# A graph network layer: projection and second neighbour sum made one stage, in the order of the places of the nodes

## The reference

```python
def _sage_conv(x, src, tgt, W_l, b_l, W_r):
    n = x.shape[0]
    msgs = x[src]
    agg = jax.ops.segment_sum(msgs, tgt, num_segments=n)
    deg = jax.ops.segment_sum(jnp.ones((src.shape[0],), x.dtype), tgt, num_segments=n)
    agg = agg / jnp.maximum(deg, 1.0)[:, None]
    return agg @ W_l + b_l + x @ W_r
h = jax.nn.relu(_sage_conv(x, src, tgt, W_l1, b1, W_r1))
logits = _sage_conv(h, src, tgt, W_l2, b2, W_r2)
```

## Time and profile before

| | us |
|---|---|
| three runs | 2976.88, 2973.86, 2979.23 |
| median | 2976.88 |
| profiled execution, own time | 2971.24 |
| its span in the trace | 2969.0 |
| PE busy in the span | 2485.4 |
| DVE busy | 2065.8 |
| POOL busy | 1809.9 |
| ACT busy | 779.7 |

### The profile page before, as it was taken

One profiled execution on the slowest core, in us unless ns is written; L12 is line 12 of the kernel. 1 busy time (PEld: TensorE's weight loads), 2 busy tenths in 40 slices (PEclk: granted clock), 3 DMA queues, 4 the chain that ended last, 5 costly groups with the idle time before them and its releaser, 6 DMA issues. The chain is left out here.

```text
span 2969.0 us, 35216 instructions
## 1 busy us (share of the span) xinstructions
PE 2485.4 (84%) x8644; PEld 1445.1 (49%) x8644; DVE 2065.8 (70%) x4653; ACT 779.7 (26%) x2019; POOL 1809.9 (61%) x1880
## 2 busy tenths in 40 slices
PE   5478888799999999989998858888777777787899
PEld 2133334245555555546666545555343444443577
DVE  8999999977777777744535656666654444444888
ACT  1011111067777767743222310000010000000232
POOL 4777776767676767740037757777547777777200
PEclk8789999889999999999999979999888777776799
DMA  9212222469999999982057665556343333333001
GB/s 267 84 56 77 83 72 87 149 183 267 265 268 263 264 267 263 267 247 95 26 154 201 201 195 169 168 169 169 96 135 106 105 106 106 105 106 105 22 1 45
DMA packets 238393, 446.46 MB, mean 150 GB/s; under 512 B 47451, under 2 KB 129005, under 8 KB 237999
## 3 DMA queue, kind: packets, MB, share of 16 engines
q0 software_dynamic: 96288, 254.83, 32.3%
q1 hardware_dynamic: 136416, 184.09, 19.0%
q10 hardware_dynamic: 5488, 5.28, 0.6%
HBM read 320.06 MB, written 126.13 MB: 150 GB/s over the span
## 5 line engine op out<-in xcount | busy, mean ns | idle before, releaser
L1746 POOL DMA_INDIRECT nbr_yg<-y_d,gidx x763 | 721.9, 946 | 243.6 <-PE nbr_sum L1856 124.9
L1856 PE MATMUL nbr_sum<-nbr_yg,nbr_hot 128*128 128x258 f32 x1526 | 599.9, 501 | 221.9 <-DMA nbr_yg<-y_d,gidx 175.2
L1794 DVE TENSOR_TENSOR nbr<-nbr_sum,nbr 128x258 f32 x763 | 323.5, 424 | 434.0 <-PE nbr_sum L1856 415.0
L855 POOL DMA_INDIRECT qg<-q_d,rb x480 | 480.0, 1000 | 205.5 <-DVE hb L941 102.8
L1856 PEld LDWEIGHTS nbr_sum<-nbr_yg,nbr_hot 128*128 128x128 f32 x1526 | 297.6, 231 | 507.7 <-DMA nbr_yg<-y_d,gidx 198.2
L410 POOL DMA_INDIRECT recs_d<-recs,slot_src x416 | 409.5, 984 | 164.4 <-issue 130.2
L972 PE MATMUL p_sum<-hb,wide 128*96 128x512 f32 x960 | 450.8, 591 | 0.1
L901 ACT ACTIVATE hb<-hb 128x512 f32<-128x512 f32 x480 | 296.7, 630 | 202.2 <-DVE hb L941 199.3
L941 DVE TENSOR_TENSOR hb<-p_h,qg 128x512 f32<-128x512 f32 x480 | 312.4, 680 | 26.5 <-DMA qg<-q_d,rb 21.6
L1244 POOL DMA_INDIRECT n_ahead<-y_d,gidx x165 | 158.1, 958 | 265.6 <-DMA y_d<-n_y 198.6
L698 PE MATMUL acc<-col_hot,lane_hot 128*128 128x464 f16 x832 | 205.2, 409 | 117.1 <-DVE lane_hot L645 117.1
(11 more groups left out here) (320 smaller groups left out, 3381.7 us busy)
## 6 DMA issues: line engine op xcount, KB each, us to landing
agg_d<-agg SPq DMA_DIRECT2D x240, 192.4 KB, 5.4
msg_d<-n_ahead SPq DMA_DIRECT2D x165, 128.0 KB, 2.9
nbr_ys<-msg_d SPq DMA_DIRECT2D x165, 128.0 KB, 2.7
nbr_yg<-y_d,gidx POOLq DMA_INDIRECT x763, 2.8
p_low<-p_d SPq DMA_DIRECT2D x11, 768.0 KB, 12.3
recs_d<-fill SPq DMA_DIRECT2D x16, 510.0 KB, 17.1
rb<-recs_d SPq DMA_DIRECT2D x60, 136.0 KB
qg<-q_d,rb POOLq DMA_INDIRECT x480, 5.7
```

The source lines that it names most:

```text
L855: pool.indirect_dma_start(qg[t % QB][:, :], None, S.q[:, :], bass.IndirectOffsetOnAxis(ap=rb[n % RB][:, t % BT, 1:2].bitcast(U32), axis=0) ...
L1746: pool.indirect_dma_start(yg[n % YB][:, 0:D], None, S.y[:, :], bass.IndirectOffsetOnAxis(ap=C.gidx[:, FROM + n:FROM + n + 1], axis=0)).the ...
L1794: dve.tensor_tensor(nbr, p_sum[t % SUMS][:, 0:W], nbr, ALU.add).then_inc(s_acc, 1)
L1856: pe.matmul(p_sum[t % SUMS][:, 0:W], hot[t // BT % HOTS][:, column, :], rows[:, :], start=True, stop=True).then_inc(s_sum, 1)
```

## The change

stage_project and the second call of stage_neighbours become one stage, stage_second_neighbours; stage_neighbours is kept for the first layer alone, as stage_first_neighbours.

- The projection goes by place, not by tile. z of the first layer is written by place, so ACT needs no numbers there. DVE loads chunk_at and five tile_at numbers ahead of every fifth mean, copies the chunk's reciprocals of the degrees to rdeg_at, and reads C.nbr at the tile's number. SP needs no numbers; it stores y at p.
- POOL waits for the stores of the first ten tiles of y, gathers the first 165 edge tiles out of these rows, then waits for all 25 stores and gathers the rest. It has 18 buffers instead of six, and three gathers share a semaphore; PE waits for three at a time. The semaphores of the gathers go on counting from the first layer.
- DVE makes three one-hots inside the projection, after products 2, 6 and 10. ACT, not DVE, zeroes C.nbr, after its last copy to xT.
- h and x have five buffers instead of six. The PSUM banks of the projection's rings serve as the six banks of the sums.
- PE takes the first sum behind the last projection product. SP issues the last stage's weights behind the stores of y, and clears the projection's semaphores after addition 166.
- The second layer adds z and x2 in the order of places: x2 at a fixed place, z written at a loaded tile number.

```diff
-                for tile in range(NT if layer == 0 else 0):
-                    if tile % CH == 0:
-                        own = load_own_buckets(nc, act, C.tile_at[:, tile:tile + CH], NT - 1)
-                    act.wait_ge(s_z, tile + 1)
-                    act.activation(C.z[:, bass.ds(own[tile % CH], 1), :].rearrange("p a d -> p (a d)"), p_z[:, 0:D],
-                                   ACT.Copy).then_inc(s_z_taken, 1)
+                for place in range(NT):
+                    act.wait_ge(s_z, place + 1)
+                    act.activation(C.z[:, place, :], p_z[:, 0:D], ACT.Copy).then_inc(s_z_taken, 1)
...
+def stage_second_neighbours(nc, C, A, S):
+        HB, XB, YB, MEANS, RELUS = 5, 5, 6, 5, 4
+        BT, GB, PER, HOTS, SUMS, EVERY = 8, 18, 3, 3, 6, 16
+        HOT_AFTER = {2: 0, 6: 1, 10: 2}
...
+            def _(sp):
+                for p in range(NT):
+                    sp.wait_ge(out.empty, p + 1)
+                    sp.dma_start(S.y[p * P:(p + 1) * P, :], y[p % YB][:, :]).then_inc(s_yst[p % YB], 16)
...
+                sp.wait_ge(s_last, 16 * 6)
+                sp.wait_ge(s_acc, NSTORED + 1)
+                for sem in of_projection:
+                    sp.sem_clear(sem)
...
+            def _(pool):
+                for b in range(GB):
+                    pool.memset(yg[b][:, D:W], 1.0).then_inc(s_zero, 1)
+                for b in range(YB):
+                    pool.wait_ge(s_yst[b], 16 * len(range(b, EARLY_NODES // P, YB)))
+                for t in range(NTILE):
+                    if t == NSTORED:
+                        for b in range(YB):
+                            pool.wait_ge(s_yst[b], 16 * len(range(b, NT, YB)))
+                    if t >= GB:
+                        pool.wait_ge(s_sum, t - GB + 1)
+                        pool.nop(nofuse=True)
+                    pool.indirect_dma_start(yg[t % GB][:, 0:D], None, S.y[0:EARLY_NODES, :] if t < NSTORED else S.y[:, :],
+                                            bass.IndirectOffsetOnAxis(ap=C.gidx[:, t:t + 1], axis=0)
+                                            ).then_inc(s_gath[t // PER % len(s_gath)], 16)
...
+                act.wait_ge(s_h, NT)
+                act.activation(C.nbr[:, :, :], C.zeros_w[:, 0:W].rearrange("p (a n) -> p a n", a=1).to_broadcast([P, NT, W]),
+                               ACT.Copy).then_inc(s_nbr_zero, 1)
...
+                def mean(p):
+                    if p % CH == 0:
+                        c = load_own_buckets(nc, dve, C.chunk_at[:, p // CH:p // CH + 1], NCH - 1)[0]
+                        tiles.extend(load_own_buckets(nc, dve, C.tile_at[:, p:p + CH], NT - 1))
+                        dve.tensor_copy(rdeg_at[:, p // CH, :],
+                                        C.rdeg[:, :, :].rearrange("p (c a) b -> p c (a b)", a=CH)[:, bass.ds(c, 1), :]
+                                        .rearrange("p a n -> p (a n)")).then_inc(s_deg_at, 1)
+                        dve.wait_ge(s_deg_at, p // CH + 1)
+                    if p >= HB:
+                        dve.wait_ge(s_x, p - HB + 1)
+                    nbr = C.nbr[:, bass.ds(tiles[p], 1), 0:D].rearrange("p a d -> p (a d)")
+                    dve.scalar_tensor_tensor(out=h[p % HB][:, :], in0=nbr, scalar=rdeg_at[:, p // CH, p % CH:p % CH + 1],
+                                             in1=C.z[:, p, :], op0=ALU.mult, op1=ALU.add).then_inc(s_h, 1)
...
+                for p in range(MEANS):
+                    mean(p)
+                dve.tensor_copy(p_iota[:, 0, :], C.iota_f[:, :]).then_inc(s_iota, 1)
+                dve.wait_ge(s_iota, 1)
+                for p in range(NT):
+                    product(p)
+                    if p + MEANS < NT:
+                        mean(p + MEANS)
+                    if p in HOT_AFTER:
+                        one_hot(HOT_AFTER[p])
+                dve.wait_ge(s_nbr_zero, 1)
+                for t in range(NTILE):
...
+            def _(pe):
...
+                pe.wait_ge(s_zero, GB)
+                for t in range(NTILE):
...
+                    if t == len(tr.banks):
+                        pe.wait_ge(out.empty, NT)
+                    if t >= SUMS and t % 2 == 0:
+                        pe.wait_ge(s_acc, t - SUMS + 2)
+                    if t % PER == 0:
+                        b = t // PER % len(s_gath)
+                        pe.wait_ge(s_gath[b], C.gathered[b] + 16 * (PER * (t // GB) + min(PER, NTILE - t)))
+                    pe.matmul(p_sum[t % SUMS][:, 0:W], hot[t // BT % HOTS][:, t % BT, :], yg[t % GB][:, :], start=True,
+                              stop=True).then_inc(s_sum, 1)
```

More of the change, by code:

```diff
@@ L1568, in stage_nodes, with stage_first_neighbours @@
         m.clear_sems()
-def stage_project(nc, C, A, S):
+def stage_first_neighbours(nc, C, A, S):
     with ExitStack() as ctx:
[L1576 to L1661, removed]
@@ L1664, in stage_neighbours @@
[L1664 to L1669, removed]
+        m = Mem(nc, ctx, "nbr0_")
         BT = 8
@@ L1675, in stage_neighbours @@
         assert EVERY * NT < NTILE
-        KB = 8 if layer == 0 else 0
+        KB = 8
         yg = [m.sb(f"yg{b}", [P, W]) for b in range(YB)]
@@ L1679, in stage_neighbours @@
         hot = [m.sb(f"hot{b}", [P, BT, P]) for b in range(HOTS)]
-        of_stored = m.sb("of_stored", [P, NT, W]) if layer == 0 else None
+        of_stored = m.sb("of_stored", [P, NT, W])
         w_r, b_r = m.sb("w_r", [P, KD, D]), m.sb("b_r", [1, D])
@@ L1687, in stage_neighbours @@
         s_gath, s_back = [m.sem(f"gath{b}") for b in range(YB)], [m.sem(f"back{b}") for b in range(KB)]
+        C.s_gath, C.gathered = s_gath, [16 * len(range(b, NTILE - NSTORED, YB)) for b in range(YB)]
         STORED_AT, DIRECT_AT = (1, 3, 6), (0, 2, 4, 5, 7)
-        FROM = NSTORED if layer == 0 else 0
-        mixed = MIXED if layer == 0 else 0
+        FROM, mixed = NSTORED, MIXED
         NEW = PERIOD - STORED_PER
@@ L1717, in _ @@
             def _(sp):
[L1718 to L1727, removed]
[L1728 to L1734 removed]
+                sp.dma_start(w_r[:, :, :], rows_on_partitions(A.W_r1)).then_inc(s_w, 16)
+                sp.dma_start(b_r[:, :], A.b1.rearrange("(a n) -> a n", a=1)).then_inc(s_w, 16)
+                sp.dma_start(C.w_l2[:, :, :], rows_on_partitions(A.W_l2)).then_inc(s_last, 16)
+                sp.wait_ge(s_last, 16)
+                sp.wait_ge(s_zero, YB + KB)
+                for n in range(NSTORED):
+                    if n >= KB:
+                        sp.wait_ge(s_sum, stored(n - KB) + 1)
+                    sp.dma_start(ys[n % KB][:, 0:D], S.msg[n * P:(n + 1) * P, :]).then_inc(s_back[n % KB], 16)
             @block.gpsimd
@@ L1798, in join @@
                     dve.tensor_tensor(C.nbr[:, tile, :], C.nbr[:, tile, :], of_stored[:, tile, :], ALU.add).then_inc(s_joined, 1)
-                JOIN = PERIOD * MIXED if layer == 0 else NTILE
+                JOIN = PERIOD * MIXED
                 dve.tensor_copy(p_iota[:, 0, :], C.iota_f[:, :]).then_inc(s_nbr_zero, 1)
@@ L1814, in _ @@
                         join(t - JOIN, t)
-                    tile, at = divmod(t - 2, EVERY)
-                    if layer == 1 and at == EVERY - 1 and 0 <= tile < NT:
-                        dve.wait_ge(s_z, tile + 1)
-                        place = load_own_buckets(nc, dve, C.place_of[:, tile:tile + 1], NT - 1)[0]
-                        dve.tensor_tensor(C.z[:, tile, :], p_z[:, 0:D],
-                                          C.x2[:, bass.ds(place, 1), :].rearrange("p a d -> p (a d)"), ALU.add
-                                          ).then_inc(s_z_taken, 1)
                     n, at = divmod(t, BT)
@@ L1824, in _ @@
                         one_hot(n + 2)
-                if layer == 0:
-                    for tile in range(NTILE - JOIN, NT):
-                        join(tile, NTILE - 1)
+                for tile in range(NTILE - JOIN, NT):
+                    join(tile, NTILE - 1)
             @block.tensor
```

135 lines of the change are left out of this document (122 added, 13 removed).

## The result

The changed kernel takes 2962.11 us (median of 8 runs, 2958.27 to 2968.77), the kernel before beside it 2977.37 (8 runs). The ratio is 0.9951 [0.9941, 0.9961], 15 us or 0.5% faster. Forecast were 2964.3 us and faster. The profiled execution of the changed kernel took 2958.27 us, 2956.5 of it span; forecast were 2958.6 and 2956.4.

A forecast was written before the change was run, and what follows sets the result against it. POOL's issue of gathers was taken as the bound; -13.9 us (earlier first gather) + 1.0 (tail) + 0.3 (gathers beside DVE) = -12.6 us, so 2964.3 us against the median 2976.88, range 2956 to 2972.

The forecast's parts named there:

- first gather: POOL's first gather of the second layer starts at 2165.2 instead of 2179.09, 13.9 us earlier (2161.3 to 2167.3).
- loads, a chunk: DVE's two register-load calls before every fifth mean cost 1.5 us, with the copy of rdeg 1.7 us a chunk.
- a one-hot, on the path: Each one-hot DVE makes after products 2, 6 and 10 adds 0.6 us to the projection (0.3 to 0.9).
- tenth copy of y: Three chunks of loads and two one-hots ahead of the tenth store in the projection delay it by 6.3 us.
- tenth copy to first gather: From tile ten copied at 2156.6, via a store landing 1.7 us after issue, to POOL's start at 2158.9, before added delays.
- ring at gather 19: POOL's 18 buffers last until 2187.7 and PE's first sum is done at 2187: no stall, by 0.7 us.
- zeroing by ACT: ACT zeroes 6450 columns of the table after its last copy to xT in 6.6 us, done at 2190.3.
- pace: POOL's issue of gathers in the second layer bounds it at 1.252 us each: 0.945 us instruction, about 0.305 idle.
- gathers beside DVE: Early gathers run beside DVE means reading two SBUF tables: +0.3 us over 18 gathers, between 0 and 4.5.
- last gather to last addition: At the layer's end PE sums the last two tiles together after the last gather landed: +1.0 us.
- the slower projection: Rival 2: PE's clock falls in the projection and port conflicts add, gain shrinks 4 to 8 us, about 2970; chance 0.15.
- PE did not become the bound: Rival 4: PE, summing in threes at low clock, takes 22.2 us per 16 tiles against POOL's 20.0: 3007; chance 0.04.

The follow-up runs named there:

- the undo: The changed kernel, but POOL waits for all 25 stores of y before its first gather: 2983.82 us on a quick chip, ratio 1.0022 to the kernel before.
- the two versions with cheaper loads: The changed kernel with projection register loads replaced by constants, 2956.23 us; or with loads spread singly and one-hots after products 20, 21 and 22, 2956.82 us.

## Why the prediction was right

Point by point, by its own steps:

| step | forecast | measured |
|---|---|---|
| first gather | 2165.2 (-13.9) | 2165.88 (-13.2) |
| loads, a chunk | 1.7 us | 1.8 on DVE; 1.6 by taking them out |
| a one-hot, on the path | 0.6 | 0.5 |
| tenth copy of y | +6.3 | +6.6 (2162.81) |
| tenth copy to first gather | 2.7 | 3.07; a store lands after 1.9, was 1.7 |
| last copy of y | near 2186 | 2186.69 |
| ring at gather 19 | no stall, by 0.7 us | no stall, with about 2 us to spare |
| zeroing by ACT | 6.6 us, done at 2190.3 | 5.57 us, done at 2189.95 |
| first addition | about 2190 | 2190.76 |
| pace | 1.252 | 1.252 (0.9 us of old waits gone, 0.9 of longer gathers in their place) |
| gathers beside DVE | +0.3 (0 to 4.5) | +0.9: four of thirteen took 1.14 to 1.21 instead of 0.95 |
| last gather to last addition | +1.0 | +0.2 (4.38 against 4.17) |
| last addition to the next stage, and that stage | 0 | +1.7, -1.2 |
| span | -12.6 | -12.5 |

The frame, "start of the first gather + 463 beats + a tail", is shown on the quick chips by the undo (22.9 us of start gave 21 us of time) and by the three kernels in which the start moved another way. So the mechanism was right. That the span came out within 0.1 us is luck: -13.2 for the start, 0 for the pace, +0.2 for the tail, +1.7 and -1.2 behind the layer make -12.5, where the forecast had -13.9 + 1.0 + 0.3. Sizes inside were off and cancel. The first gather came 0.7 later than forecast: 0.3 because DVE's stage itself began 0.26 later (first instruction at 2138.96 instead of 2138.70), 0.4 between the copy and the gather. The computation of the degrees grew from 0.18 to 0.60 us, which was in no step; the loads and one-hots made up for it. The tail was too dear in the forecast: the last two sums together took 1.11 us, where the earlier trace rows have 2.36 for two. The +0.3 for gathers beside DVE was laid on top of a pace of 1.252 that the forecast took to be free of waits; it held the 0.9 us of the old ring, so in the pace nothing was lost. And two terms were not in the sum at all. The next stage's first work comes 2.03 us after the last addition, not 0.32 as before, so it begins only 11.3 us earlier; the last stage then took 204.1 us, 1.2 less than before. The first of these is not explained: it was 1.54 to 2.12 in the undo and the two versions with cheaper loads, but 0.32 with twelve buffers, whose code of that stage is the same. So it is no fixed price of the change; no run isolated it.

Of the rivals, the slower projection came in a small part: the granted clock there was 0.89 instead of 1.00, and a few products took 1.6 to 2.1 us, but the tenth copy was 6.6 us late against 6.3 forecast. PE did not become the bound on the quick chips; there its busy time in the layer fell (see the last section).

The longer gathers follow one pattern. A gather that starts while a mean is running takes longer by what is left of that mean, less about 0.12 us: 0.32 left and 0.20 longer at 2168.39, 0.33 and 0.19 at 2176.09, 0.38 and 0.26 at 2178.79, 0.39 and 0.26 at 2181.55. The four longer gathers in the ring of twelve and the two beside the joins of the earlier trace rows (0.37 and 0.24; 0.30 and 0.18) fit it too. A mean that starts 0.24 us into a gather changes neither; nor did the one-hot that was running when the second gather started at 2167.14. Two gathers with the mean at each:

```profile
2169.84 0.95 POOL L1804 DMA_INDIRECT nbr_yg<-y_d,gidx  x1 [0.30 <-issue]
2170.08 0.48 DVE L1851 SCALAR_TENSOR_TENSOR nbr_h<-nbr,nbr_rdeg_at,z 128x256 f32<-128x256 f32 x1
...
2178.70 0.47 DVE L1851 SCALAR_TENSOR_TENSOR nbr_h<-nbr,nbr_rdeg_at,z 128x256 f32<-128x256 f32 x1
2178.79 1.21 POOL L1804 DMA_INDIRECT nbr_yg<-y_d,gidx  x1 [0.30 <-issue]
```

The Trainium skill ("SBUF — State Buffer", SBUF: two separate sides) describes an exclusive lock on a shared port pair, for a DVE operation with two SBUF inputs against a GpSimd operation that reads SBUF, held by whoever starts first for its whole instruction. The trace agrees for a gather behind a running mean, and shows no hold in the other two cases. So the rows beside the joins, which the forecast took to speak against that rule, fit it in part; the bound of 4.5 was five times too high because only four of thirteen gathers started inside a mean.

## What to carry to other kernels

Where a stream of equal beats is the bound, price a change by the start of its first beat, and then ask what has to come free before the buffers run out: here 18 buffers cover 22.5 us and the first consumer came after 20.6, twelve lost 5 us, and on the slower chip, where the projection took 56 us instead of 40 beside the early gathers, even 18 lost 14. What is moved beside an earlier stage can slow that stage, so look at its length again on every chip that counts. Register loads on the engine that closes a stage's loop cost their full length where they stand between its copy and its next mean, and next to nothing where that engine waits anyway; one at a time they fit into such gaps (12.12 us to the tenth copy, with and without them). What stands ahead of the tenth store counts in full, what stands behind it only against the ring.

## What the hardware showed unexpectedly

- PE's granted clock differed between versions of the ring. On the quick chip, in the second layer, PE was busy 60 to 62 of 100 us at a granted clock of 0.89, 0.83 and 0.83 (windows from 2202, 2402, 2602), where single waits had 73 to 79 at 0.82, 0.76 and 0.75 and pairs, in the ring of twelve, 67 to 72 at 0.77, 0.76 and 0.78. The sums are the same; there waiting in threes went with more of the high level (2.4 GHz) of the clock. On the slower chip it was rather the other way round: 0.74, 0.76 and 0.73 with six buffers singly, 0.64 to 0.74 in the five traces with threes (windows from 2650, 2850, 3050). So what set the clock is open. On a quick chip the higher clock bought nothing, since POOL sets the pace.
- Two chips differ by 15% on the same kernel (2977 and 3412 us). The gathers themselves are as long on both (0.945 us); what differs in this stretch is idle time while gathers run: 1.44 us from gather to gather instead of 1.25, and a projection of 56 us instead of 40 beside them, but of 40 on both without them. What ends these idle times the thin traces of that chip don't tell; the cause stays open.
- A gather is held by what is left of a DVE mean that is running when it starts, less 0.12 us, and by nothing that starts later (above).
- A 128x6450 copy on ACT took 5.57 us, 0.86 ns a column, less than the 1.0 extrapolated from short ones.
